# Moving the gathers of a mixture-of-experts stage ahead of the output and the scatters

## The reference

```python
k = int(bs * CAPACITY) // n                      # 4096 rows / 8 experts = 512
scores = jax.nn.softmax(xf @ gate_w.T, axis=-1)
vals, idx = jax.lax.top_k(scores.T, k)
y = xf[flat_idx].reshape(k, n, d)
...
h = jnp.einsum('knd,nfd->knf', y, fc1s) + b1s
h = jax.nn.gelu(h, approximate=True)
out = jnp.einsum('knf,ndf->knd', h, fc2s) + b2s
out = out * kept_w[..., None]
xf = xf.at[flat_idx].add(out.reshape(k * n, d))
```

## Time and profile before

| | |
|---|---|
| median of 3 runs | 970.05 us (969.35 to 970.36) |
| the profiled execution's own time | 970.41 us |
| its span, first to last instruction | 968.6 us |
| granted clock of TensorE, mean over the span | 0.900 |
| TensorE matmul busy | 762.2 us, 79% |

### The profile page before, as it was taken

One profiled execution on the slowest core, in us unless ns is written; L12 is line 12 of the kernel. 1 busy time (PEld: TensorE's weight loads), 2 busy tenths in 40 slices (PEclk: granted clock), 3 DMA queues, 4 the chain that ended last, 5 costly groups with the idle time before them and its releaser, 6 DMA issues.

```text
span 968.6 us, 15201 instructions
## 1 busy us (share of the span) xinstructions
PE 762.2 (79%) x5561; PEld 581.5 (60%) x5561; DVE 595.6 (61%) x1426; ACT 410.6 (42%) x594; POOL 352.9 (36%) x299
## 2 busy tenths in 40 slices
PE   5578999999999999999999967211459989999900
PEld 2345856767767758668577656211348888888800
DVE  2722735857857957848758562588836656666445
ACT  2632634735636536637447321100045434455324
POOL 3136333514416405425335151100134444544346
PEclk9798999999999999999999979555569999999955
DMA  7000010011011020110100102220053555555274
GB/s 208 1 23 1 1 45 1 2 66 46 23 44 44 22 84 3 48 61 0 65 23 1 66 23 83 71 94 0 7 169 92 153 132 170 138 132 135 31 213 150
DMA packets 61530, 64.63 MB, mean 67 GB/s; under 512 B 9264, under 2 KB 58160, under 8 KB 61488
## 3 DMA queue, kind: packets, MB, share of 16 engines
q1 hardware_dynamic: 54384, 55.37, 17.4%
q0 software_dynamic: 6144, 8.52, 5.0%
q10 hardware_dynamic: 960, 0.17, 0.1%
HBM read 42.95 MB, written 21.10 MB: 66 GB/s over the span
## 4 chain that ended last, share of the span: by engine, by line
PE 62%; DVE 13%; DMA 6%; ACT 6%; POOL 6%; issue 5%; POOLq 0%; DVEq 0%; SPq 0%; ACTq 0%
PE pF L1382 10%; PE pX L1660 10%; PE pF L1424 9%; PE pA L1368 6%; PE pA L1375 5%; PE pX L1464 5%; DMA xg<-row_scratch,idx_g 4%; PE pX L1393 4%; PE pA L1353 3%; DVE qe L1108 3%; PE pX L1382 3%; POOL xg L799 2%; PE pA L1434 2%; PE pF L1477 2%; PE pF L1353 2%
## 5 line engine op out<-in xcount | busy, mean ns | idle before, releaser
L1424 PE MATMUL pF<-w,h 128*128 128x256 f32 x512 | 116.0, 380 | 0.0
L1424 PEld LDWEIGHTS pF<-w,h 128*128 128x128 f32 x512 | 95.6, 190 | 13.8 <-issue 1.4
L719 POOL TENSOR_SCALAR ve<-mv 128x4 f32<-128x4 f32 x40 | 9.1, 228 | 247.0 <-DVE mv L861 246.4
L807 POOL DMA_INDIRECT acc_scratch<-at,idx_s x32 | 51.6, 1613 | 107.3 <-DVE at L1216 100.6
L799 POOL DMA_INDIRECT xg<-row_scratch,idx_g x32 | 47.3, 1478 | 99.0 <-issue 86.0
L630 ACT ACTIVATE h<-pX,b1cur 128x512 f32<-128x512 f32 x64 | 44.1, 690 | 88.9 <-DVE b1cur L1227 75.4
L1660 PE MATMUL pX<-w_lo,h_hi 128*128 128x256 f32 x256 | 73.7, 288 | 0.8 <-issue 0.8
L1660 PE MATMUL pX<-w_hi,h_lo 128*128 128x256 f32 x256 | 73.0, 285 | 0.0
L1660 PE MATMUL pX<-w_hi,h_hi 128*128 128x256 f32 x256 | 72.9, 285 | 0.0
L867 DVE TENSOR_SCALAR z<-z,mv,rstd 128x256 f32<-128x256 f32 x64 | 62.3, 1034 | 7.0 <-POOL rstd L721 7.0
L479 ACT ACTIVATE h<-pF,b1c 128x512 f32<-128x512 f32 x64 | 44.2, 691 | 48.4 <-PE pF L1382 48.4
(11 more groups left out here) (260 smaller groups left out, 1860.0 us busy)
## 6 DMA issues: line engine op xcount, KB each, us to landing
kp<-fc1T SPq DMA_DIRECT2D x8, 1024.0 KB, 7.9
w<-fc2T SPq DMA_DIRECT2D x8, 1024.0 KB, 8.0
xin<-video SPq DMA_DIRECT2D x8, 512.0 KB, 3.9
x<-video SPq DMA_DIRECT2D x8, 512.0 KB, 4.5
x_scratch<-x SPq DMA_DIRECT2D x8, 512.0 KB, 2.9
acc_scratch<-xf SPq DMA_DIRECT2D x8, 512.0 KB, 3.0
row_scratch<-y SPq DMA_DIRECT2D x8, 512.0 KB, 3.0
qp<-x_scratch SPq DMA_DIRECT2D x2, 1024.0 KB, 10.5
```

The lines of the kernel that those rows point to most:

```text
L807: pool.indirect_dma_start(acc_d, bass.IndirectOffsetOnAxis(ap=idx_s[:, g:g + 1], axis=0), og[:, g, :], None, compute_op=ALU.add).then_inc( ...
L1424: ins = nc.tensor.matmul(slots[m][:, half * D:(half + 1) * D], h[:, k, tok(2 * m + half)], w2[:, k, :], start=(k == 0), stop=(k == FC - 1))
```

## The change

Three places change. SyncE's loads for expert 1 and the first part of x1 wait for the landing of the first gather, and no longer for the row numbers alone. GpSimd issues the gather of expert e+2 ahead of the four scatters of expert e, where it stood between the second and the third. VectorE makes `wnext` of e+1 and `idx_g` of e+2 as soon as it has made the last `h_lo` of expert e, ahead of `idx_s`, the split of the next weights and the output's additions, where it stood behind the first half of the output.

```diff
--- before.py
+++ after.py
@@ -433,7 +433,7 @@
                 load_expert(0)
 
                 sp.wait_ge(x1_out, 16 * B)
-                sp.wait_ge(idx_ready, 1)
+                sp.wait_ge(gathered, 16 * GT)
                 for part in range(B // 2):
                     load_expert(1 + part, part)
@@ -799,27 +799,25 @@
-            def scatter(e, tiles):
-
-                for g in tiles:
+            def scatter(e):
+
+                for g in range(GT):
                     pool.wait_ge(og_ready, e * GT + g + 1)
                     settled(pool)
...
             gather(0)
 
             def expert(e, after):
 
+                if after == 2:
+                    gather(e + 2)
                 wait(pool, scattered, e * 16 * GT)
                 pool.wait_ge(idxs_ready, e + 1)
-                scatter(e, range(GT // 2))
-                if after == 2:
-                    gather(e + 2)
-                scatter(e, range(GT // 2, GT))
+                scatter(e)
 
             gather(1)
             experts(pool, expert)
@@ -1198,6 +1196,11 @@
                     dve.wait_ge(h_hi_ready, e * FC + n + 1)
                     nc.vector.tensor_tensor(h_lo[:, n, :], h[:, n, :], h_hi[:, n, :].bitcast(F32), ALU.subtract).then_inc(h_lo_ready, 1)
 
+                if after:
+                    next_weights(e + 1)
+                    if after == 2:
+                        idx_for_gather(e + 2)
+
                 wait(dve, scattered, e * 16 * GT)
@@ -1214,10 +1217,6 @@
                     dve.wait_ge(yo_ready, e * 2 + m + 1)
                     for g in (2 * m, 2 * m + 1):
                         nc.vector.tensor_scalar(og[:, g, :], og[:, g, :], wcur[:, g:g + 1], None, ALU.mult).then_inc(og_ready, 1)
-                    if m == 0 and after:
-                        next_weights(e + 1)
-                        if after == 2:
-                            idx_for_gather(e + 2)
```

## The result

The changed kernel takes 953.92 us, the median of 4 runs (952.74 to 957.92), beside 970.20 us (969.35 to 971.01, 4 runs) for the kernel before on the same chip: a ratio of 0.984, 95% interval 0.981 to 0.9869. Forecast were 954.7 us, in a range of 953.2 to 958.6. The profiled execution took 953.77 us, 16.64 less than that of before.

A forecast was written before the change was run, and what follows sets the result against it. TensorE, waiting in the experts' stage for late gathers, was taken as the bound; 12.20 + 3.26 = 15.46 us off the profiled 970.41 gave 954.95, adjusted to the median as 954.7 us, range 953.2 to 958.6.

The forecast's parts named there:

- The steady part: Experts 1 to 6: issuing gather e+2 earlier removes the late gathers' whole cost, 12.20 us.
- The second rival: Experts 1 to 6: gathers still come late in part; half of the 12.20 us lost gives 961; chance 0.05.
- The clock within it: Experts 1 to 6: of 12.20 us, 1.6 lie beyond the waits, mostly from TensorE's clock at half after expert 2's wait.
- The first gather: Before expert 0: with loads held back, its last tile lands in 3.1 us instead of 6.36, saving 3.26 us.
- The rise of the clock: Expert 0's hidden stage: half clock moves with the work, costing 0; if its time stays, 1.5 us lost.
- The scatters: GpSimd, each expert: first two some 2.5 us late, fourth some 5 us earlier; `idx_s` wait goes, valued at nothing.
- the slow rival: Experts' stage: late scatters make `idx_s` wait beyond a free 5 us, ending slower than before; chance 0.03.
- The port rival: GpSimd's gather issues: VectorE's split slows or blocks them, until 736.28 at worst; landing 748.8, still 4.0 us ahead; chance 0.05.

The follow-up runs named there:

- the move alone: Changed kernel with SyncE's old wait, so only the gather and its row numbers move earlier: 957.74 us, 0.9868 of the kernel before.
- the hold alone: Kernel before, with only SyncE's loads of expert 1 and first part of x1 waiting for the first gather's landing: 966.62 us against 969.79, 0.9964.
- VectorE's order alone: Kernel before, with `wnext` and `idx_g` moved behind the last `h_lo`, the gather left between the scatters: 970.28 us, 0.9999.
- every load held: Kernel before, with the loads of experts 1 to 7 each waiting until that expert's gather has landed: 969.43 us, 0.999.
- GpSimd's order alone: Kernel before, with gather e+2 ahead of the scatters on GpSimd, its row numbers made where they were on VectorE: 961.71 us, 0.9914.
- the last experiment: Changed kernel, expert 0's rows turned tile by tile as they land, VectorE's first weight split held until the second tile landed: 953.32 us, 0.9826.

## Why the prediction was right

**The steady part, 12.20 us.** Measured: 12.38 us in the profiled pair, 12.1 in the times of the move alone. Each step of it can be read off. The round without a wait, put together as 23.82 us from pieces of the earlier trace rows, is 23.79. `idx_g` follows the last `h_lo` at once. The four issues take 735.10 - 729.99 = 5.11 us from first to last where 6.04 was taken. With the 6.50 us of the earlier trace rows the tile at 735.10 is there at 741.6, 8.7 us ahead of need; 7.2 were forecast. The 6.50 was the slowest of the last tiles and not the slowest landing of before: the first tile of that gather, issued at 743.26, took 8.4 us. The second rival's "slower than any seen" overlooked it. Its sum comes out the same: 742.3 + 8.4 = 750.7 is still 2.1 us ahead of 752.8.

**The clock within it.** The 1.6 us beyond the waits were put down mostly to one fall of the clock. The chain of before bears it out: the turn at 781.05 took 1.55 us where the next one took 1.10, and the output stage behind it 12.60 where the next one, at 809.05, took 11.52, together 1.5 us:

```profile
782.60 12.60 PE pX L1660 x96
```

In the profiles such falls in the experts' stage, 3.4 us long, come only where TensorE still waits for gathers: one before, two in the hold alone, two with VectorE's order alone; none in the move alone or the change. Not each such kernel has one: with every load held, and with GpSimd's order alone, there are waits and no fall. That the waits cause the falls was not tried apart.

**The first gather, 3.26 us.** Measured: the last tile landed in 2.75 us for 6.36, 3.6 us less; 3.2 us in the times of the hold alone. The bounds were 0 and 3.26, and the choice of the upper one was right; in the profile the gain is even 0.35 us above it, since the landing came out shorter than the 3.1 of the earlier trace rows. The loads then had no difficulty: the first weights, expected by 716, were issued at 708.29 and landed in 4.9 us, not 8.8, and the second gather delayed nobody (the turn has one wait). The rise of the clock moved with the work: 4.8 us at half and then full, and 13.71 us for that hidden stage against 13.61.

**The scatters.** The fourth was to go some 5 us earlier against the stages: it was issued at 743.58 for 751.14, 7.6 earlier on a schedule that is 741.55 - 739.02 = 2.5 ahead, so 5.0. The next `idx_s` at 752.90 finds it landed. That its removed wait was worth nothing holds: the chain of before does not pass through it, and moving `idx_s` behind the split in the changed kernel gives nothing.

**What the prediction had only by half.** In the slow rival it took the wait of `idx_s` as free up to 5 us, because TensorE has that much time until `x2T_lo`. That counts TensorE alone. Where `idx_g` stands behind the same split, as in the kernel before, the wait also delays the next gather and the scatters behind it, and the loop closes well below 5 us: with GpSimd's order alone, 4.3 us at most in a round cost 4 us in all. The change is safe from it because it moves `idx_g` out from behind that wait; the prediction treated VectorE's part as a cost of 0.15 us twice and did not say that the 12.20 us need both moves. The slow rival's mechanism exists, as the held loads show. In the change the fourth scatter has 9.3 us to land, from its issue at 743.58 to the next `idx_s` at 752.90: 5.6 more than the 3.71 us of the last scatter, but only 0.9 more than the slowest of the held loads' run, 8.4.

**The port rival.** The issue at 731.51 started while VectorE wrote `w_lo`, which took from 730.42 to 732.71, and ended at 733.54, 0.83 us behind it; with VectorE idle an issue takes 0.95 or 0.96 (701.74 and 703.01 in the last experiment). So it was held until `w_lo` was through, and no longer: `x2T_lo` follows `w_lo` at once and didn't hold it further. The same stands in the slow issue of before, 744.94 + 2.72 = 747.66, 0.82 us behind the end of the `w_lo` of the other weights:

```profile
744.55 2.29 DVE L1243 TENSOR_TENSOR w_lo<-w,w_hi 128x2048 fp32r<-128x2048 f32 x1
```

The prediction read this as a slowing and set a block of the whole stretch against it, to `x2T_lo`'s end at 736.28; both were wrong. It is a block, but by one long instruction at a time, at most 2.29 us here. The issue at 729.99 began inside `w_hi` and ended at 731.20, though `w_lo` had begun at 730.42. By the Trainium skill, SBUF — State Buffer, section "SBUF: two separate sides", whichever of the two starts first, GpSimd's instruction or such a one of VectorE with two inputs in SBUF, holds the shared pair for its whole instruction. These rows agree in that the hold ends with VectorE's instruction, which the prediction's account left out. One row agrees less, the last issue of the last experiment: it began at 704.26, ahead of `w_hi`, and still ended at 705.85, behind it:

```profile
704.51 1.23 DVE L1241 CAST w_hi<-kp 128x2048 fp32r<-128x2048 f32 x1 [5.35 <-DMA xg<-row_scratch,idx_g]
```

Neither reading touched the sum, as said there.

**The size.** 954.7 against 953.92: the sum, 15.46, is 0.5 us under the 15.98 of its two terms in the profiles. No term was left out that the runs show to be the change's.

## To carry to other kernels

When a transfer is moved ahead in one engine's queue, move the instruction that makes its addresses too: either half alone gave nothing or two thirds of the move's gain here. For each wait in an in-order queue, list all that is queued behind it and follow each item round to the same wait in the next round; if the loop's time is over the bound engine's round, the loop sets the pace though the bound engine seems to have room. Holding bulk loads behind a small urgent transfer pays where no other urgent one follows (3.2 us once at the start), and not where they then meet one (with every load held, nothing was left of the 3.2).

## What was not expected of the hardware

- An accumulating scatter of 128 rows landed in 3.71 us with no load beside it, and in 7.4 to 8.4 us in the run with every load held, where 1 MB loads are issued within a microsecond of it. That is 2.0 to 2.3 times as long; the gather's last tile, 6.36 against 2.75 us, is 2.3 times.
- A gather's issue on GpSimd takes 0.95 us with VectorE idle, and the very first one 1.24 (the last experiment). In the 13 profiles 96 such issues begin inside a `w_lo` of 128x2048, and all end 0.81 to 0.91 us behind it, so they cost 1.5 to 2.8 us by how early in `w_lo` they start. Those that begin up to 0.45 us ahead of a `w_hi`, 21 of them, end 0.11 to 0.13 us behind it, and the nine that begin 0.63 us or more ahead go through in 0.94 to 1.04. Moving the split moved the long issue with it, from the second (1.64) to the last (1.59).
- Behind five of the waits for a late gather TensorE's clock was at half for 3.4 us, in three profiles (one, two and two). In the kernel before, that stretch cost 1.5 us.
